# Moving the dt times x copies of a state-space scan from VectorE to ScalarE, with three smaller reorderings

## The reference

```python
h = layernorm(x) * (1 + scale) + shift          # modulation by the condition
h = h[:, perm]                                  # steps in another order
xm, z = split(h @ W_in)                         # 512 channels each
xm = silu(conv4(xm) + conv_b)                   # causal, over 4 steps
dtr, B, C = split(xm @ W_xp)                    # 64, 16, 16
dt = softplus(dtr @ W_dt + b_dt)
# for each step t: 128 sequences x 512 channels x 16 states
hst = hst * exp(dt_t * A) + (dt_t * x_t) * B_t
y_t = sum(hst * C_t over the 16 states)
out = x + gate * (((y + xm * D) * silu(z)) @ W_out)[:, inv_perm]
```

## Time and profile before

| | |
|---|---|
| median of 3 runs | 1981.66 us (1980.7 to 1988.88) |
| profiled execution, its own time | 1983.11 us |
| its span, first to last instruction | 1979.6 us |
| mean granted TensorE clock | 0.986 |
| VectorE busy | 1841.2 us, 93% |
| TensorE matmul busy | 1828.8 us, 92% |
| ScalarE busy | 1706.3 us, 86% |
| GpSimd busy | 1659.6 us, 84% |

### The profile page before, as it was taken

One profiled execution on the slowest core, in us unless ns is written; L12 is line 12 of the kernel. 1 busy time (PEld: TensorE's weight loads), 2 busy tenths in 40 slices (PEclk: granted clock), 3 DMA queues, 4 the chain that ended last, 5 costly groups with the idle time before them and its releaser, 6 DMA issues. The chain is left out here.

```text
span 1979.6 us, 43161 instructions
## 1 busy us (share of the span) xinstructions
PE 1828.8 (92%) x12641; PEld 1424.4 (72%) x12641; DVE 1841.2 (93%) x3623; ACT 1706.3 (86%) x4011; POOL 1659.6 (84%) x1867
## 2 busy tenths in 40 slices
PE   6999999985899999999999999999999999999873
PEld 4666666662577878787877878787877878787773
DVE  5999999884899999999999999999999999999997
ACT  3777777773999999999999999999999999999881
POOL 3677777784699999999999999999999899998581
PEclk9999999997999999999999999999999999999997
DMA  6122222212000000000000000000000000001264
GB/s 173 60 68 75 75 67 76 70 58 69 1 12 12 12 12 17 9 15 18 12 12 12 12 12 17 7 17 17 12 12 12 12 12 12 12 6 49 65 224 186
DMA packets 71482, 80.82 MB, mean 41 GB/s; under 512 B 12243, under 2 KB 63699, under 8 KB 69204
## 3 DMA queue, kind: packets, MB, share of 16 engines
q1 hardware_dynamic: 69024, 70.67, 11.3%
q10 hardware_dynamic: 2228, 7.41, 1.0%
HBM read 44.46 MB, written 33.59 MB: 39 GB/s over the span
## 5 line engine op out<-in xcount | busy, mean ns | idle before, releaser
L829 ACT ACTIVATE decay<-dtT,decay_rate 128x256 f32<-128x256 f32 x2048 | 864.9, 495 | 0.6
L705 PE MATMUL bank<-ident,decay 128*128 128x128 f32 x4096 | 612.9, 273 | 46.1 <-DVE state L966 23.3
L705 PEld LDWEIGHTS bank<-ident,decay 128*128 128x128 f32 x4096 | 477.6, 142 | 104.9 <-ACT decay L829 63.4
L720 PEld LDWEIGHTS bank<-ident,scaled 128*128 128x128 f32 x3496 | 415.1, 141 | 179.7 <-issue 147.0
L720 PE MATMUL bank<-ident,scaled 128*128 128x128 f32 x3496 | 529.0, 274 | 1.1 <-POOL scaled L613 0.2
L966 DVE SCALAR_TENSOR_TENSOR state<-dtx,bc,bank 128x512 f32<-128x512 f32 x512 | 357.2, 738 | 0.0
L966 DVE SCALAR_TENSOR_TENSOR fresh<-dtx,bc,bank 128x512 f32<-128x512 f32 x512 | 357.2, 738 | 0.0
L956 DVE TENSOR_TENSOR bank<-bank,state 128x512 f32<-128x512 f32 x512 | 337.3, 691 | 18.7 <-PE bank L705 15.0
L956 DVE TENSOR_TENSOR bank<-bank,fresh 128x512 f32<-128x512 f32 x512 | 335.7, 690 | 14.1 <-PE bank L705 9.3
L613 POOL TENSOR_SCALAR scaled<-state,bc 128x512 f32<-128x512 f32 x378 | 260.7, 696 | 71.2 <-DVE state L966 43.4
L613 POOL TENSOR_SCALAR scaled<-fresh,bc 128x512 f32<-128x512 f32 x381 | 263.9, 696 | 39.9 <-DVE fresh L966 27.7
(11 more groups left out here) (163 smaller groups left out, 3177.8 us busy)
## 6 DMA issues: line engine op xcount, KB each, us to landing
xt<-in_x_dram SPq DMA_DIRECT2D x64, 128.0 KB, 2.5
resid<-x SPq DMA_DIRECT2D x64, 128.0 KB, 2.6
normed<-xh SPq DMA_DIRECT2D x64, 128.0 KB, 2.8
fin_r<-resid SPq DMA_DIRECT2D x8, 1024.0 KB, 5.0
xg<-normed SPq DMA_DIRECT2D x60, 128.0 KB, 2.1
ssm_out<-yo SPq DMA_DIRECT2D x30, 256.0 KB, 2.0
tap_bcT<-ssm_out SPq DMA_DIRECT2D x44, 128.0 KB, 2.2
mneg<-mask_rows SPq DMA_DIRECT2D x64, 64.0 KB, 2.8
```

The lines of the kernel that those rows point to most:

```text
L705: mm = pe.transpose(dec_bank[i % DECAY_BANKS][:, m * P:(m + 1) * P], decay[:, i // BLOCK % 2, n % GROUP, m, t % HALF * P:(t % HALF + 1) * ...
L720: mm = pe.matmul(y_bank[t % HALF][:, m * P:(m + 1) * P], scaled[:, i % RING, m * P:(m + 1) * P], ident[:, :], is_transpose=True, start=Fal ...
L829: act.activation(decay[:, block % 2, e // CB, m, :], dtT[c % 2][:, m, half * HTOK:(half + 1) * HTOK], ACT.Exp, scale=decay_rate[:, m, n:n ...
```

## The change

Four edits:
1. The 62 copies x0 to x3 that lie in the scan's loops go from VectorE to ScalarE (the two of chunk 0 that come first stay on VectorE). On ScalarE they stand in the slot after the fill, behind that slot's decays.
2. `rows` no longer waits for its own write and no longer raises `s_yo`. The store on SyncE waits on the side bank's semaphore instead, and so does VectorE before the final rows.
3. SyncE loads the first eight row numbers in one instruction, before it waits for the last rows of the attention block.
4. At the start ScalarE runs silu of chunk 0 and what follows it ahead of the moves of chunk 1's u0 and u1; VectorE takes z0 and z1 ahead of chunk 1's first taps.

```diff
         def mamba_sync(sp):
+            sp.wait_ge(s_order, 4)
+            first_rows = loaded_order(order, 0, 2 * T, mybir.EngineType.SP, STEPS - 1)
             attention_over(sp)
-            sp.wait_ge(s_order, 4)
...
-                    row = sp.value_load(order[0:1, bass.ds(c * T + t, 1)], min_val=0, max_val=STEPS - 1)
+                    if c < 2:
+                        row = first_rows[c * T + t]
+                    else:
+                        row = sp.value_load(order[0:1, bass.ds(c * T + t, 1)], min_val=0, max_val=STEPS - 1)
...
             def store_rows(c, q):
 
-                sp.wait_ge(s_yo, c * 2 + q + 1)
+                moved(sp, c, f"out{q}")
...
+            def copy_x(k, t):
+
+                filled(act, k, f"x{t}")
+                reached(act, s_state, (k - 1) * ITEMS)
+                act.activation(dtx[k % 2][:, t, :], side_of(k, f"x{t}")[:, :], ACT.Copy)\
+                    .then_inc(s_side_moved[side_turn(k, f"x{t}")[0]], 1)
...
+                for t in range(T):
+                    k = chunk_at(c, i, X_COPY[t])
+                    if k is not None:
+                        copy_x(k, t)
...
             for k, job in FIRST:
-                if job == "dtr":
-                    silu_x(k)
+                if (k, job) == (1, "u0"):
+                    silu_x(0)
...
-                moved(ve, k, job)
-                ve.sem_inc(s_yo, 1)
...
-                    for t in range(T):
-                        k = chunk_at(c, s, X_COPY[t])
-                        if k is not None:
-                            copy_x(k, t)
...
-            for m in range(HALF):
-                first_taps(1, m, s_tap_v)
             for k, job in BY_VECTOR:
                 if job == "z2":
                     first_softplus()
                 first_move(k, job)
+                if job == "z1":
+                    for m in range(HALF):
+                        first_taps(1, m, s_tap_v)
...
-            ve.wait_ge(s_yo, 2 * CHUNKS)
+            for q in range(2):
+                moved(ve, CHUNKS - 1, f"out{q}")
```

More of the change, by code:

```diff
@@ L284, in build @@
         s_gated = sem("y_gated")
-        s_yo = sem("y_rows_ready")
         s_y_out = [sem(f"y_rows_stored{i}") for i in range(2)]
```

## The result

| | before | changed |
|---|---|---|
| median, beside each other on one chip | 1986.06 us (six runs, 1980.7 to 1988.88) | 1967.89 us (six runs, 1966.62 to 1970.66) |
| ratio, 95% interval | | 0.9915 [0.9899, 0.9931] |
| profiled execution / span | 1983.11 / 1979.6 us | 1967.15 / 1965.2 us |

Forecast were 1967.0 us and, between the two profiled executions, 14.6 less; measured 14.4 less in the span (15.96 less in the executions' own times, since 3.5 us lay around the span before and 1.95 after). The runs give 0.69 to 1.01%, 14 to 20 us. The kernel before stood at 1981.66 in the three runs from which I started; in the later runs beside my experiments (21, 7 and 1 of them) its medians were 1984.4 to 1986.3. So the forecast time was hit partly by luck: from the median of all six runs, 1986.06, the same 14.6 would have given 1971.5, against 1967.89 measured.

What follows compares the result with a forecast made beforehand. VectorE was taken to bound the scan at borders, TensorE's own work elsewhere. Savings 9.5 + 0.2 + 2.2 + 2.5 + 0.2 = 14.6 us turn 1983.1 into 1968.5, less 1.45 for the median: 1967.0; range 1957 to 1980.

Steps and rivals of the forecast that it cites:

- The bound and the two points: At a border VectorE sets the pace, from catching up with TensorE at 1050.24 to TensorE's waiting turn at 1062.68.
- The steady border: Per scan border: x2's 0.60 plus out0's own-write wait 0.21, less 0.13 for TensorE awaiting x0's copy: 0.68 us saved.
- Fourteen equal borders: The scan's 14 borders each save the same 0.68 us, 9.5 us in all, bounds 4.3 to 11.3.
- ScalarE's cover: ScalarE's 2.54 us of waits before silu cover four copies' 1.92 per chunk, 0.62 left, so silu starts no later.
- Chunk 0: Its own x2 and x3 leave VectorE, worth about 1.2, but ScalarE is late next: 0.2 us saved, bounds -0.5 to 1.2.
- The last border: VectorE bounds all of it, so x0, x1, x2 and both row waits count: 2.2 us saved, bounds 0.8 to 2.6.
- The gather: At the start, early row numbers let the DMAs issue earlier and closer together: 2.5 us saved, bounds 0.9 to 2.6.
- Silu first: At the start, silu ahead of the moves lets TensorE's dtr start earlier: 0.2 us saved, bounds -0.3 to 0.9.
- The clock's 0.6: At the first products, a clock rise tied to time would cost up to 0.6 us of the gather's gain; not booked.
- the first (all of TensorE's idle time goes): Rival in the scan: TensorE's 1.48 us idle goes at 14 borders, 20.7, total 25.8 saved, 1955.9 us; 1 in 10.
- The second: Rival: ScalarE's x0 copy is late ahead of out0, 0.7 us in place of 0.13; priced at 1977 us; 2 in 10.
- The third: Rival: ScalarE becomes the loop's bound, its waits not shrinking; half case priced +10.7 us, 1992; 1 in 10.

Runs made afterwards that it cites:

- Three copies alone: Kernel before with copies x0, x1 and x3 on ScalarE, x2 left on VectorE, rows as they were: period 89.92 us, ratio 1.0004.
- x2 alone: Changed kernel with x0, x1 and x3 back on VectorE and only x2 on ScalarE: period 88.90 us, ratio 0.9908.
- x0 early: Changed kernel with ScalarE's copies of x0 and x1 ahead of their slot's four decays: period 88.89 us, ratio 0.9904.
- x2 and x3 twice: Changed kernel with ScalarE's copies of x2 and x3 made twice, the second after the first is written: period 89.00 us, one run.
- The gather alone: Kernel before with only the early load of the first eight row numbers: period 89.85 us, 1523.0 us behind attention, one run.

## Why the prediction was right, step by step

- *The bound and the two points.* Right. VectorE counts only between its catching up behind out0's pieces and the turn that waits. Three copies alone gave +0.14, x2 alone the whole.
- *The steady border*, forecast 0.68: measured 0.77. x2's 0.60 and x0's price held (0.14 for 0.13 forecast, and twice the copy made it 0.61 more). The mis-sized term is the rows' 0.21, which is 0.30. The bracket shows the idle time, but without the wait the next instruction also overlaps with the rows: the starts moved together by 0.29, and alone the edit took 0.30 from the border stretch. 0.60 + 0.30 - 0.14 = 0.76 is what the changed kernel's border stretch lost, and without x0's price (17.14) it lost the whole 0.90.
- *Fourteen equal borders* were thirteen. The first gave 0.39 only (gate to gate 89.40 against 89.79): `out0` waits 0.27 for the copy there. In two kernels without that wait the first border is like the others (88.89 with x2 alone and with x0 early). Why ScalarE's copy comes later at this border isn't shown; with x2 and x3 twice it had more to do in chunk 0, and the first border was like the others. Sum of the fourteen: 0.39 + 13 x 0.77 = 10.4, forecast 9.5.
- *ScalarE's cover.* Right: forecast 0.62 left ahead of silu after the copies, measured 13.4 / 14 = 0.96, so the wait fell to about half and not, as the prediction's sign had it, to a third. Its wait of 0.79 for a feed is gone; no turn of TensorE in a steady chunk waited for a decay.
- *Chunk 0*, forecast 0.2: dtr to the chunk's second gate took 74.80 in place of 74.86, so 0.06. The turn that now waits 0.89 for ScalarE's decay at 534.74 is the lateness that was named.
- *The last border*, forecast 2.2: 87.11 to 84.71, so 2.4, of it 1.8 by the copies and 0.6 by the rows in the runs with one of them.
- *The gather*, forecast 2.5: 2.1 in this profile, 2.5 over eight executions. The single parts: 0.9 by the load (from the landing of the last stored row to the first DMA it was 1.14, 461.47 to 462.61, and is 0.23, 462.29 to 462.52), 1.76 by the spacing, and 0.1 to 0.5 given back by the last landing. The first modulation started at 466.87 and not near 465.7 as forecast: 0.8 of that is the longer attention block, 0.4 the late landing.
- *Silu first*, forecast 0.2 with bounds -0.3 and 0.9: 0.4 by the run with it alone, for the reason given: dtr's bank waits for the moved move. Where the clock rose late it was up to 1.3, above the upper bound.
- *The clock's 0.6*, put at nothing. The pair of traces can't tell: the group of sixteen first products took 8.66 to 10.02 us over the executions as the clock came from 0.50 to 1.00 at differing moments, and that scatter is larger than the term. All thirteen together can tell a little. Counted from the last statistics of the attention block, the clock rose after 20.3 to 23.0 us in the five executions without the gather's edit (mean 21.7) and after 17.8 to 20.4 in the eight with it (mean 19.4). So the rise came 2.3 earlier, with products that came 2.5 earlier, and the sixteen products were on average only 0.1 longer, less than their scatter. The rule that the prediction takes from the Trainium skill, "TensorE: Matmul & The Clock Gate", Part 1, that activity releases the throttle, would have the rise move along with the products, and these traces agree.
- *The tail*, forecast 0: 0.4 was lost behind the last border (67.46 to 67.90 us). The kernels whose last period is 84.7 have 67.7 to 67.9 there, the others 67.4 to 67.8. The gather alone, whose scan and tail are those of before, has 67.81, so this may be no more than scatter between executions; no run settles it.

Together: 2.1 + 0.6 (dtr after the modulation, 25.02 to 24.37, silu and clock together) + 0.1 + 10.4 + 2.4 - 0.4 = 15.2 behind attention, less 0.8 by which the attention block was longer: 14.4. Forecast 14.6. That the two lie 0.2 apart is luck in part: the borders were forecast 1.1 too low, and the tail's 0.4 and the attention block's 0.8, neither of them forecast, took it back.

Of the rivals, the first (all of TensorE's idle time goes) fails. Its 1.48 were the brackets; by the distances of the starts TensorE lost 1.33 and 0.47 at its two waits, 1.80 in all, and of these 0.64 (bracket 0.42) and 0.17 are left, beside the new 0.14. The second needed 0.7 ahead of out0, and it was 0.14. The third did not come: in steady chunks 1.22 us more of ScalarE's work a chunk still cost nothing, and with 2.44 more the loop was slower than before. The rule of the Trainium skill on the copy ("VectorE: DVE Perf Modes", section on the TRN2 errata) gives an estimate of 0.57 for each; the length here is 0.57 to 0.60, but the distances say 0.48 where independent work follows, and 0.61 where the next instruction waits for it.

## What to carry to other kernels

In a loop like this one, where three engines are each over 95% busy, look for the stretch between the point where the bounding engine last waited for the other and the next turn that waits for it: only work inside it counts. Here moving the one copy of that stretch gave more than moving all four (border stretch 17.14 against 17.28), and the three that lay outside made the loop slower. When such a move frees a buffer from another engine, see whether the copy stands early enough in its new queue: the same 0.6 us were free at one place of ScalarE's queue and cost TensorE 0.61 at another.

## What the runs showed of the hardware that I had not expected

- A wait for the engine's own write costs more than its bracket: VectorE's 0.21 was 0.29 from start to start, since the overlap with the next instruction goes as well. ScalarE's copy was 0.48 with independent work behind and 0.61 with a wait for its write.
- An unchanged attention block of some 456 us ended 6.3 us apart in thirteen executions (455.50 to 461.79), while the scan's periods agreed within 0.05 us in an execution and, with one and the same loop, within 0.07 between executions. For small effects in a loop a profile's period tells more than repeated run times, and the length of the very stretch that was changed tells more than the period.
- Register loads ahead of DMA issues on SyncE cost 1.12 a row from issue to issue, against 0.54 with the numbers in registers. With four rows issued so closely the last landed 2.10 to 2.63 after its issue, where it was 2.04 to 2.11.
